# Audio tower on one core: projection, keys and values in the successor's round, and products of ones in TensorE's waits

## What is computed

```python
h = einsum('bg,egp->bep', x, weight * mask) + bias          # x 64x5000, weight 16x5000x128 -> h 64x16x128
h = h + attention(layernorm(h))       # 8 heads, causal over the 16 tokens of a row, low-rank q and kv, rope
h = h + experts(layernorm(h))         # 64 experts, the best 2 of each token by sigmoid scores, plus a shared one
# attention: cq = LN(x @ W_dq); q = [cq @ W_uq, rope(cq @ W_qr)]; ckv = LN(x @ W_dkv); K, V = ckv @ W_ukv
#            k = [K, rope(x @ W_kr)]; softmax(q k / sqrt(18)) V @ W_o.T
# experts: 2.5 * p_i / (p_1 + p_2) weighs silu(x w1) * (x w3) @ w2 of the token's two experts
```

## Time and profile before

| | us |
|---|---|
| median of three timed runs | 243.42 |
| lowest, highest | 242.53, 243.67 |
| profiled execution | 243.9 |
| its span, first to last instruction | 242.2 |
| busy in the span: TensorE, VectorE, GpSimd, ScalarE | 184.0, 151.8, 145.2, 83.2 |
| mean granted clock of TensorE | 0.908 |

### The profile page before, as it was taken

How to read it: one execution, slowest core, us unless ns; L and a number is a source line. 1 busy time by engine, 2 the same in 40 slices (tenths; PEclk the granted TensorE clock), 3 DMA queues, 4 the chain that set the end, 5 groups by cost and what they waited for, 6 DMA issues and landing times.

```text
span 242.2 us, 6074 instructions
## 1 busy us (share of the span) xinstructions
PE 184.0 (76%) x2479; PEld 151.4 (63%) x2479; DVE 151.8 (63%) x366; ACT 83.2 (34%) x245; POOL 145.2 (60%) x117
## 2 busy tenths in 40 slices
PE   0047967558989979979769669678999999999710
PEld 0046956456878968858658548455788778768410
DVE  0014385586487886897996976979876749101391
ACT  2005200003334323243152143346549764345500
POOL 3316469619998959979979949502054261176360
PEclk9999999977999989999999999955559999999965
DMA  6989999999999999999999999939801237433341
GB/s 210 285 295 421 353 414 395 334 422 415 420 414 416 423 420 420 413 426 418 407 389 221 216 217 200 145 91 306 229 1 34 84 104 210 142 100 89 110 98 47
DMA packets 32981, 65.11 MB, mean 269 GB/s; under 512 B 2874, under 2 KB 25367, under 8 KB 32375
## 3 DMA queue, kind: packets, MB, share of 16 engines
q1 hardware_dynamic: 31416, 59.47, 74.2%
q10 hardware_dynamic: 576, 3.26, 3.4%
q0 software_dynamic: 960, 1.97, 2.9%
HBM read 56.96 MB, written 7.73 MB: 267 GB/s over the span
## 4 chain that ended last, share of the span: by engine, by line
PE 41%; DVE 20%; DMA 11%; SPq 9%; ACT 8%; issue 5%; POOL 2%; POOLq 1%; ACTq 0%; DVEq 0%
PE bank L850 12%; DMA ring<-in_L_tok_weight_dram 9%; PE bank L1015 5%; DVE ring L1234 5%; SPq L370 4%; DVE bank L1262 4%; PE bank L1044 4%; DVE prod L1255 3%; PE bank L1027 2%; SPq L376 2%; PE bank L893 2%; PE bank L991 2%; PE bank L901 2%; PE bank L997 2%; DVE prod L1284 2%
## 5 line engine op out<-in xcount | busy, mean ns | idle before, releaser
L474 POOL TENSOR_TENSOR ring<-ring,mask 128x896 f32<-128x896 f32 (+1 forms) x48 | 91.6, 1935 | 19.6 <-DMA ring<-in_L_tok_weight_dram 19.5
L850 PE MATMUL bank<-ring,xT 128*64 128x128 f32 x1248 | 83.3, 291 | 12.3 <-DVE ring L1234 8.1
L850 PEld LDWEIGHTS bank<-ring,xT 128*64 128x64 f32 x1248 | 75.0, 147 | 17.6 <-DVE ring L1234 12.6
L1234 DVE TENSOR_TENSOR ring<-ring,bank 128x1024 f32<-128x1024 f32 (+1 forms) x45 | 45.7, 1048 | 36.0 <-DMA ring<-in_L_tok_weight_dram 36.0
L463 POOL TENSOR_TENSOR rstd<-mv,half 128x1 f32<-128x1 f32 (+1 forms) x24 | 14.3, 601 | 30.0 <-DVE mv L1242 23.1
L541 POOL DMA_INDIRECT ring<-expert_outputs,slot_index x16 | 16.1, 1003 | 16.7 <-DMA expert_outputs<-ring 12.5
L494 POOL DMA_INDIRECT expert_inputs<-xf,slot_index x14 | 14.3, 1022 | 5.9 <-DVE slot_index L1344 2.7
L831 PE MATMUL bank<-cst,w 64*128 64x64 f32 x39 | 5.3, 328 | 16.4 <-DMA w<-in_x_dram 15.7
L516 POOL TENSOR_TENSOR mask<-ring,mask 128x256 f32<-128x256 f32 x8 | 7.1, 890 | 17.0 <-ACT ring L711 17.0
L1015 PE MATMUL bank<-w,ring 128*64 128x128 f32 (+1 forms) x256 | 14.8, 296 | 0.6 <-ACT ring L711 0.6
L831 PEld LDWEIGHTS bank<-cst,w 64*128 64x128 f32 x39 | 5.0, 219 | 16.5 <-issue 15.7
(11 more groups left out here) (151 smaller groups left out, 294.0 us busy)
## 6 DMA issues: line engine op xcount, KB each, us to landing
ring<-in_L_tok_weight_dram SPq DMA_DIRECT2D x48, 832.0 KB, 13.0
expert_inputs<-w ACTq DMA_DIRECT2D x3, 1024.0 KB, 10.0
ring<-expert_inputs SPq DMA_DIRECT2D x6, 512.0 KB, 5.7
expert_outputs<-ring SPq DMA_DIRECT2D x12, 256.0 KB, 2.6
mask<-in_L_tok_mask_dram SPq DMA_DIRECT2D x3, 832.0 KB, 16.4
w<-in_x_dram SPq DMA_DIRECT2D x1, 1250.0 KB, 13.9
w2p<-in_L_ffn_w_dram SPq DMA_DIRECT2D x1, 1024.0 KB, 18.7
xT<-masks_dram SPq DMA_DIRECT2D x1, 1024.0 KB, 7.7
```

The lines of the kernel that those rows point to most:

```text
L474: pool.tensor_tensor(unit(j, q, SPLIT(q // 2), UC), unit(j, q, SPLIT(q // 2), UC), mask[:, (m + SPLIT(q // 2)) * D:(m + UC) * D], ALU.mult ...
L850: last = pe.matmul(bank[0][64 * par:64 * par + 64, 0:D], xT[:, (UC * t + c) * B:(UC * t + c + 1) * B], unit(j, 2 * t + par, c, c + 1), sta ...
L1234: dve.tensor_tensor(both(j, t, a, b), both(j, t, a, b), m.rearrange("p (u f) -> p u f", u=1).to_broadcast([P, 2, (b - a) * D]), ALU.mult). ...
```

## The change

Projection, keys and values of chunk c-1 (not c-2) run in round c; chunk 0's run in round 2, ahead of chunk 1's. VectorE begins a round with stats_h(c-1) and multiply_keys(c-2). The order of masks, roots and of the steps on each engine is written anew, and heads(5) moves into round 7. In the tail only chunk 7 is left to project. `spin(n)` issues n products of a 128x128 tile of ones by 512 columns of ones (bf16) into bank[1], 26 in all, all ahead of up(0). Left out of the diff below are the two constants that fall away and the first line of TensorE's loop.

```diff
@@ -496,15 +494,25 @@
                         in_=xf[:, j, :], in_offset=None, bounds_check=ROWS[j // NCH1] - 1, oob_is_err=False).then_inc(s_scat[j // NCH1], 16)
 
             for c in range(NCH):
-                b, d = c - 2, c - 3
-                mask_pieces(POOL_SHARE[0])
-                if d >= 0:
+                a, d = c - 1, c - 3
+                if c < 2:
+                    mask_pieces(UNITS)
+                    if c == 1:
+                        root_h(0)
+                elif c == 2:
+                    mask_pieces(2)
+                    root_qk(0)
+                    root_h(1)
+                    mask_pieces(3)
+                    root_qk(1)
+                    mask_pieces(1)
+                else:
+                    mask_pieces(2)
+                    root_h(a)
                     root_h2(d)
-                if b >= 0:
-                    root_qk(b)
-                mask_pieces(POOL_SHARE[1])
-                if c >= 1:
-                    root_h(c - 1)
+                    mask_pieces(2)
+                    root_qk(a)
+                    mask_pieces(2)
                 for j in SCATTERED.get(c, ()):
                     scatter(j)
 
@@ -518,10 +526,9 @@
             scatter(NCH1 - 1)
             pool.wait_ge(s_pmask, UNITS * NCH)
             j, k, l = NCH - 3, NCH - 2, NCH - 1
-            root_qk(k)
             root_h(l)
+            root_h2(j)
             root_qk(l)
-            root_h2(j)
             mid(0)
             mid(1)
             root_h2(k)
@@ -676,24 +683,35 @@
                     act.dma_start(xs_dram[1].rearrange("(p r) d -> p (r d)", p=P), zeros).then_inc(s_zero[1], 16)
                 if d >= 0:
                     copy_oT(d)
-                if b >= 0:
-                    copy_xnT(b)
-                    square_qk(b)
+                if c == 1:
+                    norm_h(0)
+                if c == 2:
+                    copy_xnT(0)
+                    square_qk(0)
+                    norm_qk(0)
+                    turned_qk(0)
+                    heads_k(0)
+                    heads_v(0)
+                if a >= 1:
+                    norm_h(a)
                 if d >= 0:
                     norm_xf(d)
-                if b >= 0:
-                    norm_qk(b)
+                if a >= 1:
+                    copy_xnT(a)
                 if d >= 0:
                     copy_xfT(d)
-                if b >= 0:
-                    copy_qkv(b)
-                if c == NCH - 1:
-                    norm_h(a)
-                    copy_xnT(a)
-                if b >= 0:
+                if a >= 1:
+                    square_qk(a)
+                if c == 2:
+                    probs(0)
+                if a >= 1:
+                    norm_qk(a)
+                    turned_qk(a)
+                if b >= 1:
                     probs(b)
-                if 0 <= a < NCH - 2:
-                    norm_h(a)
+                if a >= 1:
+                    heads_k(a)
+                    heads_v(a)
 
             def copy_xsT(g):
                 act.wait_ge(s_t1, g + 1)
@@ -732,26 +750,21 @@
 
             j, k, l = NCH - 3, NCH - 2, NCH - 1
             keep_h(l)
-            square_qk(k)
+            copy_oT(j)
+            norm_h(l)
+            copy_xnT(l)
+            square_qk(l)
+            norm_xf(j)
+            norm_qk(l)
+            copy_xfT(j)
+            turned_qk(l)
+            probs(k)
             score_exp(0, NCH1)
-            norm_qk(k)
-            turned_qk(k)
-            norm_h(l)
-            heads_k(k)
-            copy_xnT(l)
-            copy_oT(j)
-            square_qk(l)
-            heads_v(k)
-            norm_qk(l)
+            heads_k(l)
             copy_xsT(0)
-            probs(k)
-            turned_qk(l)
+            heads_v(l)
             copy_xsT(1)
-            norm_xf(j)
-            heads_k(l)
-            copy_xfT(j)
             silu(0)
-            heads_v(l)
             copy_xsT(2)
             copy_oT(k)
             silu(1)
@@ -942,40 +955,55 @@
                     pe.wait_ge(s_rope, 2)
                     pe.wait_ge(s_qw, 16 * 6)
                     pe.wait_ge(s_centred, 2)
-                project_b, attend_d = b >= 0, d >= 0
                 ahead = 2 if c >= SUMS_AHEAD else 0
                 for n in range(ahead):
                     sum_genes(c, n)
-                if attend_d:
+                if c == 2:
+                    turn_xn(0)
+                    project(0)
+                if d >= 0:
                     turn_o(d)
-                if project_b:
-                    turn_xn(b)
-                if attend_d:
                     attend(d)
-                if project_b:
-                    project(b)
                 for n in range(ahead, 4):
                     sum_genes(c, n)
-                if attend_d:
+                if c == 2:
+                    turn_qk(0)
+                sum_genes(c, 4)
+                if c == 2:
+                    qkv(0)
+                    sum_genes(c, 5)
+                    values(0)
+                if a >= 1:
+                    turn_xn(a)
+                if d >= 0:
                     turn_xf(d)
-                if project_b:
-                    turn_qk(b)
-                sum_genes(c, 4)
-                if attend_d:
+                if a >= 1:
+                    project(a)
+                if d >= 0:
                     gate(d)
-                if project_b:
-                    qkv(b)
-                if attend_d:
+                for n in range(6 if c == 2 else 5, 8):
+                    sum_genes(c, n)
+                if d >= 0:
                     rank_tokens(d)
-                sum_genes(c, 5)
-                if project_b:
-                    values(b)
-                for n in range(6, 12):
-                    sum_genes(c, n)
-                    if c == NCH - 1 and n == 10:
-                        turn_xn(c - 1)
-                if c == NCH - 1:
-                    project(c - 1)
+                sum_genes(c, 8)
+                if c == 2:
+                    sum_genes(c, 9)
+                if a >= 1:
+                    turn_qk(a)
+                if c != 2:
+                    sum_genes(c, 9)
+                if a >= 1:
+                    qkv(a)
+                sum_genes(c, 10)
+                if a >= 1:
+                    values(a)
+                sum_genes(c, 11)
+
+            def spin(n):
+
+                for _ in range(n):
+                    pe.matmul(bank[1][:].rearrange("p (a n) -> p a n", a=4), ones[:],
+                              ones[:].rearrange("p (a n) -> p a n", a=1).to_broadcast([P, 4, P]), start=True, stop=True)
 
             def turn_xs(g):
                 if g % 2 == 0:
@@ -1064,21 +1092,25 @@
                 last.then_inc(s_sh2, 1)
 
             j, k, l = NCH - 3, NCH - 2, NCH - 1
-            turn_qk(k)
-            qkv(k)
+            turn_o(j)
+            spin(2)
+            attend(j)
+            spin(7)
             turn_xn(l)
-            turn_o(j)
+            spin(2)
             project(l)
-            values(k)
-            attend(j)
+            spin(6)
+            turn_xf(j)
+            turn_qk(l)
+            spin(3)
+            gate(j)
+            qkv(l)
+            spin(4)
             turn_xs(0)
-            turn_qk(l)
+            values(l)
+            spin(2)
             turn_xs(1)
-            qkv(l)
-            turn_xf(j)
             up(0)
-            gate(j)
-            values(l)
             turn_xs(2)
             turn_o(k)
             up(1)
@@ -1358,32 +1390,41 @@
 
 
                 a, b, d = c - 1, c - 2, c - 3
-                mask_pieces(VECTOR_SHARE[0])
-                if d >= 0:
-                    add_attended(d)
                 if c == 1:
+                    mask_pieces(2)
                     turn_rope()
                     centre_projections()
-                mask_pieces(VECTOR_SHARE[1])
+                    mask_pieces(1)
+                    stats_h(0)
+                    mask_pieces(3)
+                    continue
                 if c == 0:
+                    mask_pieces(3)
                     dve.wait_ge(s_rem, 32)
                     dve.wait_ge(s_mrem, 16)
                     dve.tensor_tensor(wrem[0:GREM], wrem[0:GREM],
                                       mrem[0:GREM, :].rearrange("p (a n) -> p a n", a=1).to_broadcast([GREM, S, D]),
                                       ALU.mult).then_inc(s_remm, 1)
-                mask_pieces(VECTOR_SHARE[2])
-                if d >= 0:
+                    mask_pieces(3)
+                    continue
+                stats_h(a)
+                if c == 2:
+                    mask_pieces(3)
+                    multiply_keys(b)
+                else:
+                    multiply_keys(b)
+                    add_attended(d)
+                    mask_pieces(3)
                     choose(d)
-                if a >= 0:
-                    stats_h(a)
```

(21 more changed lines are left out.)

## The result

| | before | after |
|---|---|---|
| median of four timed runs, us | 243.14 | 255.82 |
| profiled execution, us | 243.9 | 254.69 |
| its span, us | 242.2 | 253.0 |
| mean granted clock | 0.908 | 0.927 |

The ratio is 1.0518 (95% interval 1.0471 to 1.0565). I had forecast 248.3 in a range of 242 to 254: the direction came, the size did not. The profiled execution is the lowest of its four, and that of before lies just above its four, so between the profiles the difference is 10.8 us of span and not the 12.7 of the medians.

What follows compares the result with a forecast made beforehand. The prediction took VectorE's work to bound the late rounds and the half-clock stretch from 155 to 181 us as the place to win. 6.5 + 0.7 + 1.6 - 1.1 - 2.8 = +4.9 us gave 248.3, range 242 to 254.

Steps and rivals of the forecast that it cites:

- round 2: Chunk 1's whole projection joins this round, each link waiting for the last; chunk 2 closes at 77.6, not 71.1: +6.5 us.
- round 3 and first part of 4: Chunk 3's products wait in one line, 16.1 us against 14.3; VectorE gives back 1.1 in round 4: +0.7 us.
- rounds 4 to 7, the loop: From add_attended(1) to add_attended(4): place 2.2 us late each round behind GpSimd's masks, today's waits go: +1.6 us.
- add_attended(4) to less_max(5): VectorE stretch up to less_max(5): waits and moved work leave, two masks and a 3.3 us place wait enter: -1.1 us.
- the tail: Behind less_max(5): 17.5 us to up(0) against 16.9, then up(0) to up(2) 5.9 against 9.35: -2.8 us.
- place, a term put at nothing: Place's own VectorE operations: no term of the sum lengthened them; only place's wait for the rank was counted.
- The waits in the loop: VectorE's 5.9 us of waits between add_attended(1) and add_attended(4) all go, the gate's covered by three masks.
- my bound of 8: Upper bound in us on round 2's added cost, if the clock drops in the waits.
- one: Rival: sums don't come later, since round 2's delay runs into VectorE's waits and place isn't late; 238.5 us, chance 0.14.
- two: Rival: place is late by half of what was counted; 243.3 us, chance 0.13.
- Three: Rival: the clock falls despite the spins, in the wait for heads(5) behind the last sums; 253.8 us, chance 0.13.
- Transfers: SyncE's weight requests come 6 to 10 us later, costed at nothing; if they fall behind, a round starts up to 1 us later.

Runs made afterwards that it cites:

- round 2's line alone: Changed kernel with chunk 1's line taken out of chunk 2's sums, qkv(1) and values(1) moved to round 3, rank_tokens still behind sums 5 to 7: 254.51 us, ratio 1.0519.
- the early rank alone: Changed kernel with rank_tokens(d) moved ahead of sums 6 and 7, behind sum 5, on TensorE: 246.62 us, ratio 1.0244 to the kernel before.
- both: Changed kernel with rank_tokens(d) ahead of sums 6 and 7, and chunk 1's line taken out of chunk 2's sums: 244.47 us, ratio 1.0107.

## Why the prediction was wrong in size

| step | forecast, us | measured in the profile | the same with place's operands in PSUM |
|---|---|---|---|
| round 2 | +6.5 | +7.6 | +7.8 |
| round 3 and first part of 4 | +0.7 | +2.1 | +0.1 |
| rounds 4 to 7, the loop | +1.6 | +3.1 | +2.1 |
| add_attended(4) to less_max(5) | -1.1 | -0.6 | -0.1 |
| the tail | -2.8 | -1.5 | -1.1 |
| sum | +4.9 | +10.8 | +8.7 |

- **The step that failed is place, a term put at nothing**: from round 3 to the last part I counted its operations as unchanged. The mechanism around it held: masks, sums and rank between root_h2 and place, VectorE waiting there with TensorE's rank as releaser, within 0.4 us in the loop. But beside the masks, place's two operations are longer than before by 2.8 us in round 3, 1.7 in the three loops and 0.8 in the last part; these steps are over by 1.4, 1.5 and 0.5. With the operands in PSUM the operations are short, the wait ahead of place grows, and less_max(5) ends at 164.6 instead of 167.1. I had 162.5: so by these two profiles the missing term is worth 2.5 of the 4.6 us that are over there. GpSimd's masks stood in the earlier trace rows; I asked who waits for whom, and not what would now run beside them.
- **The waits in the loop**: I let all of today's 5.9 us go, and 1.4 for the gate stayed.
- **The sum adds steps that do not add.** Undoing round 2's line alone is worth nothing that shows, the early rank alone 2.7%, both 4.1%. While place's line sets the rounds, an earlier start of round 3 turns into waits.
- **Round 2**: the 60 records took 2.3 us more at the lower clock, near my bound of 8 for that case. The other links came within some 0.4 us of my count, but the line started 1.2 earlier: up to values(0) I had said that no time moves.
- **The tail**: up(0) starts 17.5 us behind less_max(5), as forecast, and up(2) 6.2 behind up(0) against 5.9. Behind up(2) I had no difference, and there are 62.2 us instead of 61.2; the profiles of the other kernels have from 61.1 to 63.0 there, 61.1 and 61.9 in two without spins. So a difference of 1 us lies within what these profiles spread over, and I did not test what makes it.
- **Of the rivals**, one and two fall: chunk 2 did close late, and place was late in full. Three came half true: the clock was 0.52 from 168 to 174, but 1.00 again ahead of up(0), and the whole tail came out 1.3 short and not 5.5.
- **Transfers** were rightly left at nothing: behind 56 us VectorE does not wait for tok_weight in the changed kernel.

## What to carry to other kernels

When work is moved to an earlier round, ask first which engine sets that round: here TensorE set rounds 2 and 3 (and VectorE, by its small idle time, the later ones), so work that was nearly free behind the last sums cost most of its length there (2.8 of 3.45 us). When steps change places on two engines, list the pairs that now run side by side, not only the waits. Products that keep TensorE's clock up in a tail full of waits can be had without a new order, and were worth more alone than the reordering with them.

## What the hardware showed that I had not expected

A VectorE operation on two elements per partition ended only with GpSimd's running mask, 1.2 and 1.9 us instead of 0.16, with both its operands in SBUF. With one of them in PSUM it took 0.16 in the three rounds of the changed kernel that had a mask beside it. Beside GpSimd's short roots and its scatters it took no more than 0.23 from SBUF either. The Trainium skill (GPSIMD Engine Reference, section 1. Specifications) says that GpSimd shares its SBUF interfaces with VectorE, and that instructions with two SBUF inputs, or in a 2-port perf mode, contend. The trace agrees on the two inputs, and adds the size: the ends coincide, so the operation stands until the mask is over. Two SBUF operands are not the whole condition: the operation between the two, with one, was long as well, once in the kernel with the early rank and once in that with round 2's edit alone, each time to the end of a mask. Whether it ran in such a mode no trace here shows.

```profile
105.40 1.58 DVE L1375 TENSOR_SCALAR spot<-rank 128x2 f32<-128x2 f32 x1
```

```profile
86.70 1.52 DVE L1391 TENSOR_SCALAR spot<-rank 128x2 f32<-128x2 f32 x1
```

The spin's price, which no row of before had: 0.24 to 0.27 us each at the full clock (six in 1.46, three in 0.81), where I took 0.26, and about 0.5 at the lower (two in 1.06). The first of the 26 ran at the lower clock, so all took 8.2 us where I took 6.8; the 5.6 that the prediction names beside it is further off.
